# Mixture of experts on one core: order of the first gathers, the experts' parameters, and the second tile's transposes

## What is computed

```python
var = jnp.mean(x * x, axis=-1, keepdims=True)
xn = rms_w * (x * jax.lax.rsqrt(var + EPS))
gate = xn @ wg_W + wg_b + (genre_embed @ gg_W + gg_b)
gate_w = jax.nn.softmax(gate, axis=-1)
topk_w, topk_i = jax.lax.top_k(gate_w, TOP_K)
cw = jnp.sum(jax.nn.one_hot(topk_i, E, dtype=x.dtype) * topk_w[..., None], axis=-2)
h1 = jax.nn.relu(jnp.einsum('bsh,ehm->bsem', x, W1) + b1)
h2 = jax.nn.relu(jnp.einsum('bsem,emn->bsen', h1, W2) + b2)
out_e = jnp.einsum('bsen,enh->bseh', h2, W3) + b3
return jnp.einsum('bseh,bse->bsh', out_e, cw)
```

## Time and profile before

| | us |
|---|---|
| median of three runs | 482.25 |
| the three runs | 483.4, 480.2, 482.25 |
| the profiled execution | 481.19 |
| its span | 479.5 |

### The profile page before, as it was taken

The page is one execution under the profiler, slowest core; times in us unless marked ns, Lnnn a source line. Parts: engine busy times, 40 slices in busy tenths (PEclk is TensorE's granted clock), DMA queues, the critical chain, the costliest instruction groups (busy, mean ns, idle before and its releaser), DMA issues.

```text
span 479.5 us, 13384 instructions
## 1 busy us (share of the span) xinstructions
PE 431.3 (90%) x4296; PEld 385.7 (80%) x4296; DVE 306.3 (64%) x531; ACT 289.9 (60%) x608; POOL 302.3 (63%) x457
## 2 busy tenths in 40 slices
PE   7606889999899999999999999899999999999980
PEld 6406768998689889888888998788899999899870
DVE  4898734776657756856856666555566667775550
ACT  6606529877578768778777764544555556554550
POOL 5720742757777776877877776766656666666451
PEclk9956989999899999999999999999999999999997
DMA  8989692555434544240444331322323433112221
GB/s 289 352 227 377 255 327 82 129 151 135 118 71 131 135 68 122 40 68 24 60 73 115 63 61 22 69 47 46 46 46 51 56 46 47 26 24 40 35 34 19
DMA packets 27179, 49.48 MB, mean 103 GB/s; under 512 B 8267, under 2 KB 21645, under 8 KB 24941
## 3 DMA queue, kind: packets, MB, share of 16 engines
q0 software_dynamic: 13632, 18.00, 22.9%
q1 hardware_dynamic: 9280, 30.45, 18.0%
q10 hardware_dynamic: 4205, 0.17, 0.5%
HBM read 40.08 MB, written 17.83 MB: 121 GB/s over the span
## 4 chain that ended last, share of the span: by engine, by line
PE 37%; POOL 26%; issue 12%; DVE 7%; ACT 5%; POOLq 4%; DMA 2%; DVEq 1%; SPq 0%; ACTq 0%
PE bank L1226 25%; POOL out L611 11%; PE bank L1260 7%; POOL area L579 5%; POOL bound L519 2%; ACT area L756 2%; DMA stage<-in_weights 1%; POOLq L597 1%; DVE area L1025 1%; PE bank L1202 1%; POOL cfrom L574 1%; DVE area L1023 1%; PE bank L1182 1%; ACT area L770 1%; PE bank L1273 1%
## 5 line engine op out<-in xcount | busy, mean ns | idle before, releaser
L1226 PE MATMUL bank<-area,w_hi 128*128 128x256 f16 x1536 | 257.0, 275 | 6.2 <-DVE area L1025 5.8
L1226 PE MATMUL bank<-area,w_lo 128*128 128x256 f16 x768 | 210.8, 274 | 0.0
L770 ACT ACTIVATE area<-bank,cprm 128x256 f32<-128x256 f32 (+1 forms) x264 | 132.3, 556 | 78.2 <-PE bank L1226 62.1
L1226 PEld LDWEIGHTS bank<-area,w_hi 128*128 x1536 | 150.7, 99 | 26.3 <-issue 8.2
L1023 DVE CAST area<-area 128x512 f16<-128x512 f32 (+1 forms) x144 | 66.1, 459 | 137.4 <-ACT area L770 127.1
L611 POOL DMA_INDIRECT out<-area,cto x71 | 119.2, 1679 | 41.9 <-issue 29.3
L1025 DVE TENSOR_TENSOR area<-area 128x512 f16<-128x512 f32 (+1 forms) x144 | 99.0, 688 | 5.0
L579 POOL DMA_INDIRECT area<-x_ext,cfrom x65 | 69.6, 1071 | 37.7 <-POOL cfrom L574 27.9
L1260 PE MATMUL bank<-w_hi,area 128*128 x496 | 86.3, 273 | 0.0
L1226 PEld LDWEIGHTS bank<-area,w_lo 128*128 x768 | 75.8, 99 | 9.3
L780 ACT ACTIVATE area<-area,cw 128x256 f32<-128x256 f32 x71 | 32.3, 500 | 71.0 <-DVE area L1030 52.7
(11 more groups left out here) (199 smaller groups left out, 468.9 us busy)
## 6 DMA issues: line engine op xcount, KB each, us to landing
stage<-in_weights SPq DMA_DIRECT2D x10, 1024.0 KB, 6.0
area<-in_x SPq DMA_DIRECT2D x8, 512.0 KB, 7.5
x_ext<-in_x SPq DMA_DIRECT2D x8, 512.0 KB
out<-in_x SPq DMA_DIRECT2D x8, 512.0 KB, 6.9
w_lo<-in_weights SPq DMA_DIRECT2D x4, 1024.0 KB, 8.3
w_hi<-in_weights SPq DMA_DIRECT2D x2, 1024.0 KB, 9.0
out<-area,cto POOLq DMA_INDIRECT x71, 3.9
area<-x_ext,cfrom POOLq DMA_INDIRECT x65, 3.0
```

The costliest lines, as they stand in the source:

```text
L770: ins = act.activation(to[:, m * T + u * wide:m * T + (u + 1) * wide], ps_h[layer][b][:, a * T + u * wide:a * T + (u + 1) * wide], ACT.Rel ...
L1226: ins = nc.tensor.matmul(banks[m // 2][:, (m % 2) * T + u * wide:(m % 2) * T + (u + 1) * wide], weight, xp[:, cols], start=(k == 0 and n = ...
```

## The change

- Before step 0 GpSimd gathers tile 0 alone, calculates the first expert's parameters and copies them for tile 0, then gathers tile 1 and copies for it, then gathers tile 2.
- At least four tiles belong to the first expert, so tiles 0 to 3 no longer look their expert up (`FIRST` = 4); the wait for `s_names` stands at tile 4 on TensorE and GpSimd, and VectorE makes the names directly before the split of tile 0.
- Expert 1's parameters are calculated in step 1 instead of 0, and in every step with parameters they stand behind the adds instead of in front of the parameter copy.
- `weight_sums(0)` stands behind batch 5 instead of 3, and `keep_busy` only behind batches 0 to 2.
- The write of the scores into `x_ext` goes from ScalarE's queue to SyncE's, behind the first expert's loads.
- Tile 1's transposes stand inside layer 2 of tile 0, behind its first half, instead of behind layer 1.
- Tile position 33 is finished by halves too.

```diff
+FIRST = -(-LEAST // E)
...
-LOWS_AT, SQUARES_AT, SUMS_AT, HIGHS_AT, PARAMETERS_AT = {1: 2, 2: 3}, {}, {}, {0: 2, 1: 3}, {0: 1}
+LOWS_AT, SQUARES_AT, SUMS_AT, HIGHS_AT, PARAMETERS_AT = {1: 2, 2: 3}, {}, {}, {0: 2, 1: 3}, {1: 1}
...
-SUMS_BEHIND_BATCH = 3
+SUMS_BEHIND_BATCH = 5
...
+WARM_BATCHES = 3
...
-            return i + pair(i) + (1 if i > LAST - 1 else 0)
+            return i + pair(i) + max(0, i - (LAST - 2))
...
-            return paired(i) or i == LAST - 1
+            return paired(i) or i >= LAST - 2
...
                 b3_rows(e)
+                if e == 0:
+                    sp.wait_ge(s_dense, 1)
+                    for h in range(2):
+                        first = h * (N // 2 + 1)
+                        sp.dma_start(x_ext[first:first + N // 2, H:ROW].rearrange("(p j) e -> p j e", j=J),
+                                     je(dense)[h * P // 2:(h + 1) * P // 2]).then_inc(s_ext, 16)
...
             def copy_parameters(i, s):
                 experts = []
+                if i == FIRST:
+                    pool.wait_ge(s_names, 1)
                 for u in range(halves_of(i) if paired(i) else 1):
-                    e = pool.value_load(etile[0:1, bass.ds(name_at(i, u), 1)], min_val=0, max_val=E - 1)
+                    e = 0 if i < FIRST else \
+                        pool.value_load(etile[0:1, bass.ds(name_at(i, u), 1)], min_val=0, max_val=E - 1)
...
-                if late is not None:
-                    link(parameters(late))
                 if i + 2 == PAIRED_AT:
...
                 add_rows(i, s)
+                if late is not None:
+                    link(parameters(late))
...
                 gather(i, i, tab_from[:, i * SUB:(i + 1) * SUB])
-                if i == 1:
+                if i == 0:
                     pool.wait_ge(s_whole, 1)
                     pool.wait_ge(s_order, 1)
                     link(parameters(0))
-                    pool.wait_ge(s_names, 1)
-                    for n in range(2):
-                        experts_of.append(copy_parameters(n, n))
+                if i < 2:
+                    experts_of.append(copy_parameters(i, i))
...
-            act.wait_ge(s_dense, 1)
-            for h in range(2):
-                first = h * (N // 2 + 1)
-                act.dma_start(x_ext[first:first + N // 2, H:ROW].rearrange("(p j) e -> p j e", j=J),
-                              je(dense)[h * P // 2:(h + 1) * P // 2]).then_inc(s_ext, 16)
...
-            experts_of_tiles()
             low_parts(0)
+            low_parts(1, (0,))
             tables()
-            low_parts(1, (0,))
             x_low(0)
             low_parts(1, (1,))
+            experts_of_tiles()
             split(0, 0)
...
-                if b < BATCHES - 1:
+                if b < WARM_BATCHES:
                     keep_busy(WARM_BATCH, ones16[:, :], bank[6])
...
+                if i < FIRST:
+                    return [0]
+                if i == FIRST:
+                    pe.wait_ge(s_names, 1)
...
+                    if m == 1 and between is not None:
+                        between()
...
+                      between=(lambda: transpose_x(1, 1, 1)) if i == 0 else None,
...
-            pe.wait_ge(s_names, 1)
             layer1(0, weights_at(0))
-            transpose_x(1, 1, 1)
             weight_sums(1)
```

2 lines of the change are left out of this document (1 added, 1 removed).

## The result

The changed kernel takes 498.12 us (median of four runs, 497.79 to 500.56) beside 482.03 (480.2 to 483.4) of the kernel before: ratio 1.0347, 95% interval 1.0299 to 1.0395. The forecast was 484.7 with a range up to 492. The profiled execution took 498.05, span 496.4, which is 16.9 more than before. Lines have moved: L1188 is the transposes (before L1182), L1236 layers 1 and 2 (L1226), L1031 VectorE's split (L1025), L831 the low parts (L825), L528 to L545 the parameters (L519 to L536), L588 the gathers (L579), L623 the adds (L611), L776 and L786 ScalarE's activation and weighing (L770, L780), L1036 the finish of layer 3 (L1030).

A forecast was written before the change was run, and what follows sets the result against it. TensorE, busy 90%, was taken to wait for VectorE's splits and gathered rows, with GpSimd nearly as full. 481.2 - 3.5 (head) + 6.0 (parameters) = 483.7, with 1.06 to the median 484.7; own range 481 to 488, 8 in 10 475.5 to 492.

The forecast's parts named there:

- (c): Head, tile 0's rows: layer 1 starts at 57.1, 2.4 after the transposes, and layer 2 comes at about 62.2.
- (f): Head, gap before layer 2: shrinks from 2.11 to about 1, and the 1.2 GHz stretch behind goes, gain 1.75.
- The second rival: Gathers behind the parameters land 2.5 to 2.7 late in all seven steps, about four 1.2 GHz stretches: 495.8, chance 0.22.
- (a): Head, sums of squares later and fewer fillers: index table at 46.9, gain 1.1, kept at 0.5 to 1.2.
- (b): Head, GpSimd: first expert's parameters start at 51.4 and are ready near 57, so ScalarE no longer waits for them.
- term (g): Head, score write moved to SyncE's queue: pushes its next loads back, costed at 0, bounds -1 and +3.
- (d): Head, table of expert names directly before tile 0's split on VectorE: charged 0.6, layer 2 at 62.8 to 63.0.
- (e): Head, tile 1's transposes inside layer 2: 0.4 on the path; rows land by 63, needed at 65.5.
- (h): Names known in advance for four tiles save register loads on GpSimd and TensorE beside other work: 0.
- (i): End of the kernel, last full tile finished by halves: 0, bounds -0.5 and +0.3.
- The parameters behind the adds: Steady part: gathered rows late by 12.3 in seven steps, 14.0 with the clock, replacing 8.0: net +6.0.
- The clock: Behind the head, TensorE at 1.2 GHz after waits for late rows: one stretch of 1.7 added.

The follow-up runs named there:

- p8: Kernel before with only the score write moved to SyncE's queue behind the first expert's loads: 483.52 us, ratio 1.0024.
- p3: Changed kernel with the score write back on ScalarE's queue: 497.37 us, ratio 1.0295 to the kernel before.
- s2: Kernel before, own head, with parameters behind the adds (expert 1 in step 1) and the second low-part pair one step earlier: 477.17 us, ratio 0.9903.
- s4: Changed kernel with the second low-part pair one step earlier and the score write on ScalarE's queue: 475.45 us, ratio 0.9868.
- q3: Changed kernel with 160 idle matmuls ahead of tile 0's transposes instead of 96: 498.68 us, ratio 1.0303.
- s1: Changed kernel with the second low-part pair of experts 1 to 7 one step earlier, nothing left out: 477.42 us, ratio 0.9906.
- q2: Changed kernel with the second low-part pair of experts 1 to 7 replaced by memsets: 478.47 us, ratio 0.9899.

## Why the prediction was wrong, point by point

Four steps failed. In the head, step (c) took the first tile's rows to come 6.6 us after the first gather's start whatever else was on the queues, and step (f) therefore had a stretch at 1.2 GHz go where another came. Behind it, the lateness of the gathered rows was put at 12.3 us and measured 17.0, and the clock was charged for one stretch where four came. The mechanism of the large part, rows late because the parameters stand behind the adds, was right.

The second rival, late everywhere with four stretches, is what happened, and its 495.8 is close, but in part by luck: the rows were late by 2.1 us in most steps and 4.6 in one, not by 2.5 to 2.7 everywhere, which with the stretches gives 23.5 against its 25; and it still took off 3.5 for a head that gave +1.35.

- (a), (b): right in mechanism. VectorE waits 0.84 to 0.87 for the last batch in every trace with the new head, 1.66 to 2.68 with the old one; ScalarE waits for TensorE and no longer for the copy, which is done at 56.46. That the table came at 46.93, as forecast, is luck: with the same head it came as late as 50.5 in other traces.
- (c) failed in its first number: the first transposes came at 57.88, not 54.7, though the first gather started on time (48.08). Three things are in this. The second gather started 2.28 behind the first instead of 1.55, because the first one's instruction took 1.98 us instead of 1.25: VectorE's low parts now run beside it from 47.66, where before the work on the names stood (its pair began at 50.44). This is the meeting of T1 once more, in the head. The second gather then landed at 57.74, 7.4 us after its start at 50.36. In that time the DMA engines moved the second expert's chunks (share 0.99 from 54 to 56 in the window above), whose last landed at 58.68 instead of 54.56. That is term (g), the score write on SyncE's queue, where its issue took 6.14 us from 35.27: costed at 0 with a bound of +3, it cost 2.4 us of head in p8, where it stands alone, and 2.8 by p3, which takes it back. And even without that write the rows hardly follow the gather's start: in the kernel before, in s2 and in s4 the second gather landed 1.1 us behind the second expert's last chunk each time, though it had started 4.9, 4.3 and 5.3 us earlier. What ties the landing to the loads isn't shown.
- (d), (e): the names cost nothing, since VectorE was done with them at 63.92 and then waited 1.26 for ScalarE; tile 1's rows landed at 60.75 and were transposed at 70.46, in time.
- (f) had the wrong sign. The stretch behind layer 2 went, but the idle 3.99 us brought 6.8 us at 1.2 GHz over layer 1; TensorE is busy for 5.92 of them, so they cost up to 3.0, and q3, which is without them, has layer 2 1.8 earlier against the table. From transposes to layer 1 it now takes 3.4 instead of 2.4. The head gave +1.35 where I had -3.5: an error of 4.85.
- (h), (i): not tested by themselves; the sum in the section on the result closes without them.
- The parameters behind the adds: the mechanism was right row for row. Start W + 5.0 (forecast 4.7), length 6.6 (6.7), end W + 11.6 (11.4), landing W + 17.2 (16.9 to 18.1), wanted at W + 15.1 (15.4). But I took 1.5 for the four steps without a weight load, and three of them showed 2.1; I had set the difference between the steps on the loads, and the loads made none. The fourth, expert 7, waited 4.62: its adds started 2.7 behind W instead of 1.8, its second gather only at W + 15.6, the rows needed 3.6 to land instead of 2.8, and TensorE wanted them at W + 14.7 instead of W + 15.1. Together 17.0 against 12.3: an error of 4.7.
- The clock: one stretch of 1.7 forecast, four found at 6.5 us together, an error of 4.8. I had three gaps of about 2 us to go by, two of which were followed by a stretch. That ratio over seven is 4.7 stretches, and I wrote one.

The errors are 4.85 + 4.7 + 4.8 = 14.35. The forecast for the profiled execution was 483.7, and it took 498.05, which is 14.35 more. The rule that I weighed, that the loser of the port pair waits for the whole instruction (the Trainium skill, "SBUF — State Buffer", "Who interferes with whom"), was the one that carried the result. In the rows above, operations of 0.19 and 0.28 us end with VectorE's instructions after 1.29 and 2.43, and in s1, with the pair elsewhere, the same operations take 0.19 and 0.28. The one of 2.43 was held over two instructions in a row, which is more than the sentence says. Without the pair the parameters take 4.7 to 4.9 us, not the 3.8 of the prediction, and that was enough. What I failed to do with it was to ask whether the pair could be somewhere else.

## What to carry to other kernels

Moving a chain of small operations on GpSimd is a change to two lists: look up what VectorE runs at the new time, and move that too (20.7 us here). The same move of VectorE's pair without the other one lost 15 us. Judge "behind instruction X" by the time at which X comes in the trace, not by its place in the list. Where a load is let into a queue later, look at which latency-bound transfer it then meets.

## What the runs showed of the hardware

- Two low-part instructions of VectorE (two SBUF inputs, 1.24 us each) in the middle of GpSimd's parameters make them 6.6 us long instead of 4.7 (memsets in their place, q2) or 4.9 (pair elsewhere, s1). With two pairs they take 8.7; expert 1's in step 0, which met none, took 3.8. One GpSimd operation can be held over both instructions of a pair (2.43 and 2.18 us), or two operations over one each (1.29 and 1.02). A gather's instruction on GpSimd took 1.98 us beside the same kind of VectorE instruction, and 1.25 where it began without one.
- A gather of rows started at 50.36 landed 7.4 us later while the other queue's loads filled the engines (406 GB/s); the gather of step 7, started at 168.69 with less traffic, needed 2.8. The Trainium skill ("DMA: Bandwidth & Descriptors", "Queues, rings and completion order") says that each DMA engine takes turns between its queues by packets; the longer landing agrees with that, no run here shows the packets' order.
- Three waits of 2.12, 2.10 and 2.09 us on TensorE were followed by 3.4 us at 1.2 GHz, and such a stretch began inside the wait of 4.62; waits of 1.89, 1.98 and 2.18 had none. The length of the wait alone doesn't decide. Matmuls of no use in its place kept the clock at 2.4 GHz; the median fell by 3.1 us, where the stretches had cost 6.5.
